# Conditional residual kernel: one more load in place of a copy in four units, with loads, stores and x in another order

## What is computed

```python
# x (128, 128, 512), cond_8 = y (128, 8), weight (8, 512, 512), mask (512, 512), bias (512,)
masked_w = weight * mask[None, :, :]
w_bot = jnp.einsum('bg,got->bot', y, masked_w)       # one 512 x 512 matrix for each batch
out = x + jnp.einsum('bnt,bot->bno', x, w_bot) + bias
```

## Time and profile before

| | us |
|---|---|
| median of three runs | 661.93 |
| lowest and highest | 656.84, 661.96 |
| the profiled execution | 660.4 |
| its span, first to last instruction | 658.6 |
| TensorE busy | 633.7 |
| VectorE busy | 452.4 |
| ScalarE busy | 312.3 |
| GpSimd busy | 123.2 |
| its 16 DMA engines | 141.30 MB, mean 215 GB/s |

### The profile page before, as it was taken

How to read it: one execution, slowest core, us unless ns; L and a number is a source line. 1 busy time by engine, 2 the same in 40 slices (tenths; PEclk the granted TensorE clock), 3 DMA queues, 4 the chain that set the end, 5 groups by cost and what they waited for, 6 DMA issues and landing times.

```text
span 658.6 us, 18464 instructions
## 1 busy us (share of the span) xinstructions
PE 633.7 (96%) x7808; PEld 598.7 (91%) x7808; DVE 452.4 (69%) x449; ACT 312.3 (47%) x513; POOL 123.2 (19%) x95
## 2 busy tenths in 40 slices
PE   6989979999999997999999999999999999999998
PEld 2467759999999997999999999999999999999997
DVE  4976769889999763767666676766767667676521
ACT  0132216666666553555555555555555555555500
POOL 5685746445555000000000000000000000000000
PEclk9999999999999997999999999999999999999999
DMA  8979939889889995565569986555579995553122
GB/s 321 388 228 311 370 80 289 244 229 246 238 266 335 272 304 161 144 161 140 150 206 278 282 291 198 150 141 159 137 214 284 280 314 158 159 146 99 53 78 80
DMA packets 62881, 141.30 MB, mean 215 GB/s; under 512 B 7694, under 2 KB 33392, under 8 KB 52976
## 3 DMA queue, kind: packets, MB, share of 16 engines
q1 hardware_dynamic: 43856, 106.19, 54.5%
q10 hardware_dynamic: 18944, 33.93, 16.1%
HBM read 93.96 MB, written 46.14 MB: 213 GB/s over the span
## 4 chain that ended last, share of the span: by engine, by line
PE 81%; DVE 10%; DMA 3%; issue 3%; POOL 2%; ACT 0%; SPq 0%; DVEq 0%; ACTq 0%
PE ps L543 61%; PE ps L524 13%; PE ps L506 7%; DVE ring L437 5%; DVE ring L436 3%; DMA xs<-in_x 3%; DVE staged L458 1%; DVE raw L430 1%; POOL wbot L357 1%; DMA first_sb<-in_first 1%; POOL raw L348 1%; POOL parts L350 0%; DVE yblk L464 0%; ACT parts L378 0%; ACT wbot L387 0%
## 5 line engine op out<-in xcount | busy, mean ns | idle before, releaser
L543 PE MATMUL ps<-wbot,xs 128*128 128x128 f32 x4096 | 489.9, 278 | 7.8 <-DMA xs<-in_x 5.6
L543 PEld LDWEIGHTS ps<-wbot,xs 128*128 128x128 f32 x4096 | 471.1, 193 | 12.3 <-issue 6.4
L387 ACT ACTIVATE wbot<-ps 128x512 f32<-128x512 f32 x448 | 275.0, 614 | 237.6 <-PE ps L543 237.0
L458 DVE TENSOR_TENSOR staged<-ps,bias_sb 128x512 f32<-128x512 f32 x128 | 88.4, 691 | 176.9 <-PE ps L543 176.6
L437 DVE COPY ring<-ring 16x4096 bf16<-16x4096 bf16 x112 | 151.0, 1348 | 3.5
L436 DVE COPY ring<-ring 32x4096 bf16<-32x4096 bf16 x112 | 136.4, 1218 | 3.5
L524 PE MATMUL ps<-ydiag,ring 98*128 98x64 bf16 x3584 | 123.1, 193 | 8.2 <-DVE ring L437 8.2
L524 PEld LDWEIGHTS ps<-ydiag,ring 98*128 98x128 bf16 x3584 | 119.8, 98 | 10.9 <-issue 9.7
L348 POOL TENSOR_TENSOR raw<-raw,parts 128x512 f32<-128x512 f32 x32 | 49.3, 1540 | 70.4 <-ACT parts L378 70.4
L445 DVE TENSOR_TENSOR wbot<-ps,ring 128x512 f32<-128x512 f32 x64 | 43.4, 688 | 14.4 <-PE ps L506 10.0
L350 POOL TENSOR_TENSOR parts<-raw 128x512 bf16<-128x512 f32 x32 | 48.8, 1524 | 2.5
(11 more groups left out here) (10 smaller groups left out, 4.0 us busy)
## 6 DMA issues: line engine op xcount, KB each, us to landing
xs<-in_x SPq DMA_DIRECT2D x32, 1024.0 KB, 10.0
out<-staged ACTq DMA_DIRECT2D x128, 256.0 KB, 3.3
ring<-w_parts SPq DMA_DIRECT2D x112, 256.0 KB, 4.0
ring<-w_parts SPq DMA_DIRECT2D x112, 128.0 KB, 4.3
w_parts<-parts SPq DMA_DIRECT2D x32, 384.0 KB, 5.9
raw<-in_w SPq DMA_DIRECT2D x16, 512.0 KB, 8.8
ring<-in_w SPq DMA_DIRECT2D x4, 512.0 KB, 15.2
ring<-in_eye SPq DMA_DIRECT2D x112, 16.0 KB
```

Source lines behind the costliest of these rows:

```text
L387: eng.activation(chunk_place(b, k), chunk_sums(b, k), ACT.Copy).then_inc(s_ev_a, 1)
L458: eng.tensor_tensor(staged[:, n % OUTB, :].rearrange("p (b o) -> p b o", b=GB), ps2[n % S2B][:, :].rearrange("p (b o) -> p b o", b=GB), bi ...
L543: ins = eng.matmul(ps2[n % S2B][:, b * SL:(b + 1) * SL], xs[:, load % GROUPS * GB + b, k, :], at, start=(k == 0), stop=(k == KT - 1))
```

## The change

The first two edits shift when tiles 16 to 31 are made and when new x is loaded. `slot_of` and `free_before` give the six slots in another order. For bursts 16 to 47 (`thrice`), the units three to six, the second ring load brings part 1 again beside part 3, into rows 64 to 95, and VectorE's second copy is left out; the count of copies that `burst` waits for follows (`COPIES`). SP issues a burst's loads only from the step after the one that stored its last tile, and puts the stores of a step at its end. GpSimd makes the first four tiles in another order against its own additions. VectorE's copy of burst 16 moves from step 7 to step 6.

```diff
--- before.py
+++ after.py
@@ -48,7 +48,7 @@
 
 EARLY = 4
 TILES_AT = {0: (4, 5), 1: (6,), 2: (7, 8), 3: (9,), 4: (10, 11), 5: (12,), 6: (13, 14), 7: (15,),
-            **{8 + (t - 16) * 3 // 2: (t,) for t in range(16, TILES)}}
+            **{8 + (t - 16) * 7 // 5: (t,) for t in range(16, TILES)}}
 
 S1B = 6
 S2B = 2
@@ -77,7 +77,7 @@
     LAST_USE[x_load(_n)] = _n
 
 
-X_AT = {_g: LAST_USE[_g - _g % GROUPS - GROUPS] + 1 + _g % GROUPS * 8 // 5 for _g in range(GROUPS, XLOADS)}
+X_AT = {_g: LAST_USE[_g - _g % GROUPS - GROUPS] + 1 + _g % GROUPS * 9 // 7 for _g in range(GROUPS, XLOADS)}
 
 LAST_BURST = [CS - 1]
 for _n in range(STEPS):
@@ -97,7 +97,12 @@
 
 def slot_of(b):
 
-    return (b - FB + 4) % RING
+    return (4, 5, 0, 2, 3, 1)[(b - FB) % RING]
+
+
+def thrice(b):
+
+    return b < FB + SLICES * CS
 
 
 def free_before(b):
@@ -105,6 +110,8 @@
     r = b - FB
     if r < 3:
         return 0
+    if r == RING - 1:
+        return GROUPS
     last = FB - 1 if r < RING else b - RING
     return next(n for n in range(STEPS) if LAST_BURST[n + 1] >= last)
 
@@ -113,6 +120,10 @@
 
     return b < FB
 
+
+COPIES = [0] * (FB + 1)
+for _b in range(FB, BURSTS):
+    COPIES.append(COPIES[-1] + (1 if thrice(_b) else 2))
 
 V_DONE, A_DONE = [0], [0]
 for _b in range(BURSTS):
@@ -264,16 +275,20 @@
                         stored(eng, t)
                 if b >= FB + RING:
                     eng.wait_ge(s_s1, (b - RING + 1) * KT)
-                elif b >= FB + 4:
+                elif b >= FB + 5:
+                    eng.wait_ge(s_ev_v, FB * KT)
+                elif b >= FB + 3:
                     eng.wait_ge(s_s1, FB * KT)
-                elif b >= FB + 3:
-                    eng.wait_ge(s_ev_v, FB * KT)
                 ones = (KT - 1 - s) * CW // 2
                 eng.dma_start(ring[KROWS:KALL, i, :].bitcast(fp32), eye[c, :, ones:ones + BW // 2]).then_inc(s_eye[i], 16)
                 w1_w2 = scratch[h, 0:2, :, :, c % KT * BW:(c % KT + 1) * BW].rearrange("j g o c -> (j g o) c")
                 w3 = scratch[h, 2, :, :, c % KT * BW:(c % KT + 1) * BW].rearrange("g o c -> (g o) c")
+                w1_w3 = bass.AP(tensor=w1_w2.tensor, offset=w1_w2.offset, ap=[[2 * ROWS * HCOLS, 2], [HCOLS, ROWS], [1, BW]])
                 eng.dma_start(ring[0:2 * ROWS, i, :], w1_w2).then_inc(s_w12[i], 16)
-                eng.dma_start(ring[5 * ROWS:KROWS, i, :], w3).then_inc(s_w3[i], 16)
+                if thrice(b):
+                    eng.dma_start(ring[4 * ROWS:KROWS, i, :], w1_w3).then_inc(s_w3[i], 16)
+                else:
+                    eng.dma_start(ring[5 * ROWS:KROWS, i, :], w3).then_inc(s_w3[i], 16)
 
             def load_x(g):
                 at = g % GROUPS * GB
@@ -301,11 +316,9 @@
             for t in range(EARLY):
                 store_parts(t)
             loaded = FB
-            kept = EARLY
+            kept = 0
             for n in range(STEPS):
-                for t in TILES_AT.get(n - 2, ()):
-                    store_parts(t)
-                    kept = t + 1
+                kept = max((kept, EARLY if n >= 2 else 0, *(t + 1 for t in TILES_AT.get(n - 3, ()))))
                 if n + X_AHEAD < GROUPS:
                     load_x(n + X_AHEAD)
                 if n == 0:
@@ -319,6 +332,8 @@
                 for g in range(GROUPS, XLOADS):
                     if X_AT[g] == n:
                         load_x(g)
+                for t in TILES_AT.get(n - 2, ()):
+                    store_parts(t)
 
         @block.gpsimd
         def _(eng):
@@ -360,8 +375,10 @@
             eng.wait_ge(s_first, 16)
             for c in range(CS):
                 add_one(c)
-                if c >= CS - EARLY:
-                    subtract(c - CS + EARLY)
+                if c in (4, 5):
+                    subtract(c - 4)
+            subtract(2)
+            subtract(3)
             for n in range(STEPS):
                 for b in bursts_before(n):
                     if b < FB:
@@ -434,7 +451,8 @@
                 i = slot_of(b)
                 eng.wait_ge(s_w12[i], 16 * ((b - FB) // RING + 1))
                 eng.tensor_copy(ring[2 * ROWS:4 * ROWS, i, :], ring[0:2 * ROWS, i, :]).then_inc(s_dup, 1)
-                eng.tensor_copy(ring[4 * ROWS:5 * ROWS, i, :], ring[0:ROWS, i, :]).then_inc(s_dup, 1)
+                if not thrice(b):
+                    eng.tensor_copy(ring[4 * ROWS:5 * ROWS, i, :], ring[0:ROWS, i, :]).then_inc(s_dup, 1)
 
             def evict(b, k):
                 if on_vector(b, k):
@@ -476,7 +494,10 @@
                 for b in bursts_before(n):
                     for k in range(KT):
                         evict(b, k)
-                while made < BURSTS and made <= LAST_BURST[min(n + 1 + AHEAD, STEPS)]:
+                if n == GROUPS - 2:
+                    duplicate(FB)
+                    made += 1
+                while n >= GROUPS and made < BURSTS and made <= LAST_BURST[min(n + 1 + AHEAD, STEPS)]:
                     duplicate(made)
                     made += 1
                 for t in TILES_AT.get(n, ()):
@@ -516,7 +537,7 @@
                 eng.wait_ge(s_w12[i], 16 * (turn + 1))
                 eng.wait_ge(s_w3[i], 16 * (turn + 1))
                 eng.wait_ge(s_eye[i], 16 * (turn + 1))
-                eng.wait_ge(s_dup, 2 * (b - FB + 1))
+                eng.wait_ge(s_dup, COPIES[b + 1])
                 for k in range(KT):
                     at = b * KT + k
                     room(b, k)
```

## The result

| | before | after |
|---|---|---|
| median, us | 661.41 (four runs) | 786.02 (785.59 to 788.1) |
| profiled span, us | 658.6 | 783.8 |
| TensorE busy | 633.7 | 665.2 |
| VectorE busy | 452.4 | 397.3 |
| mean GB/s of DMA | 215 | 186 |

The ratio of after to before is 1.191, 95% interval 1.185 to 1.197. The kernel is 125 us slower, where 9 us faster was forecast.

What follows compares the result with a forecast made beforehand. TensorE, busy 96%, bounds the kernel; its waits (5.2 + 5.9 + 8.1 = 19.2 us) are the ceiling. DMA work leaves x15 late, so 8.6 us are gained: 660.4 to 651.8, said as 652 us, range 648 to 656.

Steps and rivals of the forecast that it cites:

- The price d of 128 KB more: DMA time each of bursts 16 to 47 pays for its wider second load: between 0 and 0.54 us, taken as 0.4.
- rival "slower": Rereading part 1 in bursts 16 to 47 makes d more than 0.94, kernel over 1% slower, 667 at d = 1; chance 0.06.
- The sign named for it: Backlog before step 30: steps over 4.59 us with L430 or L524 waiting for a DMA, raw tiles late for VectorE.
- Stores 4 and 5: On SP in step 2 they stand behind mask, x6 and ring loads: 5 us later, costed at nothing, else up to 5.
- the wait named as the sign: A wait for POOL or ScalarE before group 8 would say that stores 4 and 5 were not free.
- the 5.2 us of step 8: TensorE's wait for VectorE's copies of burst 16 goes when that copy moves to step 6: 5.2 us gained.
- The eight waits of steps 9 to 32: TensorE's waits of about 0.6 us after VectorE's tile steps go with the second copies: 5.9 us gained.
- SP's two stops: SP's waits for stores 27 and 31 before bursts 40 and 44, 11.4 us in all, remain and empty the queue.
- x15 lands: x15's landing sets the end: 244.7 instead of 253.3, 8.6 us gained.
- the lateness: x15 comes 8.5 us after TensorE wants it at 236.2; burst 44 may take 2 to 4 us of it.
- the sum: x15's landing from 154.8 us of DMA work at share 1.03, start 89.4 and 5.0 us of empty queue; kernel 652.
- The later units: x16 to x31, loaded over ten groups instead of twelve: no group waits for them, cost nothing.

Runs made afterwards that it cites:

- the rows outermost: Changed kernel with the new load's source written with 16 rows outermost and the two parts inside, so the product is wrong: 648.87 us in one run.
- four blocks: Changed kernel with the second load's source as four blocks of eight rows, 12 rows apart, so the product is wrong: 707.57 us in one run.
- the split load: Changed kernel with the second ring load of bursts 16 to 47 issued as two loads of 16 adjacent rows: 652.06 us, ratio 0.9875.
- the order-only run: Changed kernel with VectorE's second copy kept for all bursts and the second load of 128 KB as before: 654.37 us, ratio 0.9878.
- both moved: the split load with fewer extra loads, ring loads two steps behind their last store, and stores ahead of new x: 641.93 us, ratio 0.9709.
- the kernel with no second copy: Changed kernel with parts stored as 2, 1, 3, both ring loads 32 adjacent rows, for all bursts: 651.66 us, ratio 0.9865.

## Why the prediction was wrong

**What failed.** The step is "The price d of 128 KB more". It went from bytes (0.54) and landings (0) of loads of 32 and 16 adjacent rows to a load of two blocks apart, and took that as one of their kind. No row of before shows such a load; the diff does (`[2 * ROWS * HCOLS, 2]`). With it a burst's loads take 6.0 us, on two of the 16 engines, instead of 2.1 (1.7 + 0.4): for this form d is 4.3, not 0.4. For a load of adjacent rows d is 0.29 to 0.55, as said. Both ends put around d came from loads of one form, so no value between them could be this one. Only the rival "slower" (d over 0.94, held at 0.06) pointed the right way, and the reason named for it, part 1 read twice, is refuted: with the rows outermost the same rows are read at 648.87. The sign named for it did show: steps over 4.59 us, with the tiles' multiply (70.8 us) and TensorE (29.6 us) waiting for loads.

**What followed from it, and wasn't foreseen.** 6.0 us a burst is more than a step of 4.59. Stores, raw tiles and x stand in the same queue, so all of them came late, and stores most: 16.9 us from issue to landing in the median against 5.9. The rest of the 8.88 us is about what the same engines carry besides. Before, a step had 0.92 x 4.59 = 4.2 us of DMA work, of which a burst's loads were 1.7; the other 2.5 and the 6.0 make 8.5, an estimate. For four blocks it gives 3.8 + 2.5 = 6.3, and the bursts from 103.57 to 306.28 in that trace are 6.54 apart.

**Stores 4 and 5.** I called their delay free as long as it stays near 5 us, with up to 5 us if the cover goes. In the kernel after, ScalarE's cast of tile 9 waits until 80.28, 17 us later than before, because the three slow loads of bursts 16 to 18 stand ahead. GpSimd's additions come late behind its subtractions, and group 8 waits 8.56 us for them: the wait named as the sign. With the split load the cast is at 70.03, 7 us later than before, and no wait over 0.4 us comes of it.

```profile
80.28 0.63 ACT L395 ACTIVATE parts<-raw 128x512 bf16<-128x512 f32 x1 [24.31 <-DMA w_parts<-parts]
```

**What held, once the load is split.** Burst 16 starts at 92.60 (said: 93), burst 17 4.59 later: the 5.2 us of step 8. The eight waits of steps 9 to 32 are gone: 5.9. The DMA share from 91 to 244.9 is 0.99 (said: 1.03). SP's two stops remain, 22.8 us in all against 11.4. The rest of the timeline, burst of step 36 and group of step 39:

```profile
225.33 1.80 PE L547 MATMUL ps<-ydiag,ring 98*128 98x64 bf16 x32 [4.09 <-DVE ring L453]
...
244.97 5.46 PE L566 MATMUL ps<-wbot,xs 128*128 128x128 f32 x32 [3.18 <-DMA xs<-in_x]
```

x15 lands at 244.9 (said: 244.7), and burst 44 takes 4 us of the lateness (said: 2 to 4); the kernel takes 652.06 (said: 652). So the sum was right for a kernel that was not the one submitted. Its DMA work holds too: 0.99 x 153.9 = 152 us from 91 on, where the sum had 154.8 from 89.4. But the order-only run shows that the work is not all: with no extra load x15 landed at 250.0, issued behind the stop for store 31, which landed at 228.4. To add x15's landing up from the work was too simple; the stop for store 31 is a second bound, and only with both moved was the last of the 10 us had in every run.

**The later units** cost nothing, as said: from step 40 on every burst of the kernels above comes 4.59 us after the one before, but for a single one of the kernel with no second copy (5.06, at 396.69).

## What to carry to other kernels

Before a transfer is priced by its bytes, look at the outermost dimension of its source: here, with 2, 16 rows of 8 KB went one behind another on each of two engines, and in a queue that others use, all of them waited. Change the layout so that the rows are one run, put the larger dimension outermost, or issue two loads; each of the three took the 125 us back. The sign of it in a profile is a queue that is never empty with a DMA share near 0.5, and in it stretches at 0.13 (two engines) or 0.25 (four). And a copy taken off an engine that is late only in some steps is best replaced by a load only in those steps.

## What was not expected of the hardware

- One load of 256 KB took 3.8 us more of its queue in one form than in the other (6.0 against 2.2 a burst), for the same rows and bytes; 0.27 us for each 8 KB row on the busiest engine.
- Two blocks that touch in HBM, written as two, cost nothing (658.44 us); two apart cost 121 us of span (779.6 against 658.6).
- The DMA share tells how many engines a transfer runs on, where nothing else does: 0.13 for two blocks, 0.25 for four.
